# Selects between the early roots, an aggregate ahead of a scaling, and a first tap on GpSimd

## The reference

```python
x_sp = conv1d(x, conv_w, 3 taps, per channel, pad 1) + conv_b      # depthwise
x_mixed = x_sp^T @ lin_w^T + lin_b + emb.mean(0)                   # (16, 250, 128)
h = (x_mixed - mu) * rsqrt(var + 1e-5) * ln_g + ln_b

n1 = layernorm(h)
QK = (n1 @ Wq) @ (n1 @ Wk)^T
A = softmax(QK / 8); the row with the least sum of QK (of batch 0) is set to zero
h = h + A @ (n1 @ Wv)

n2 = layernorm(h)                                                  # over 128 features
h = h + tril(W2) @ gelu(tril(W1) @ n2 + b1) + b2
```

## Time and profile before

| | |
|---|---|
| median of 3 runs | 94.26 us (94.08 to 94.42) |
| profiled execution | 93.75 us |
| its span, first to last instruction | 92.0 us |
| TensorE busy | 85.0 us |
| VectorE busy | 73.6 us |
| ScalarE busy | 67.6 us |
| GpSimd busy | 54.9 us |
| granted TensorE clock | 1.000 |

### The profile page before, as it was taken

One profiled execution on the slowest core, in us unless ns is written; L12 is line 12 of the kernel. 1 busy time (PEld: TensorE's weight loads), 2 busy tenths in 40 slices (PEclk: granted clock), 3 DMA queues, 4 the chain that ended last, 5 costly groups with the idle time before them and its releaser, 6 DMA issues.

```text
span 92.0 us, 1984 instructions
## 1 busy us (share of the span) xinstructions
PE 85.0 (92%) x541; PEld 69.5 (76%) x541; DVE 73.6 (80%) x283; ACT 67.6 (73%) x241; POOL 54.9 (60%) x89
## 2 busy tenths in 40 slices
PE   5979987699999999999999999999999999999940
PEld 2446565379799989999899899989887988687730
DVE  2259999998999998999998899869769395862560
ACT  1688999999999769969787988666796735555400
POOL 5508768898856793999982079972708437460000
PEclk9999999999999999999999999999999999999999
DMA  1986000000000000000000000000000003425364
GB/s 23 218 289 200 0 0 4 4 0 0 11 0 0 0 0 0 0 7 4 4 0 0 0 0 7 0 0 0 0 0 0 0 7 111 115 69 154 108 188 150
DMA packets 3828, 3.84 MB, mean 42 GB/s; under 512 B 413, under 2 KB 3690, under 8 KB 3818
## 3 DMA queue, kind: packets, MB, share of 16 engines
q1 hardware_dynamic: 3466, 3.35, 13.1%
q10 hardware_dynamic: 352, 0.38, 1.4%
HBM read 1.68 MB, written 2.05 MB: 40 GB/s over the span
## 4 chain that ended last, share of the span: by engine, by line
PE 72%; DVE 8%; POOL 8%; DMA 3%; issue 3%; ACT 1%; POOLq 0%; DVEq 0%
PE bank_m L400 14%; PE bank_s L373 12%; PE bank_o L411 8%; PE bank_s L431 7%; PE bank_at L391 7%; PE bank_np L364 6%; PE bank_np L444 4%; PE bank_x L422 4%; POOL rstd L207 4%; DMA tok_w<-tok_dram 3%; PE bank_np L356 3%; PE bank_at L444 3%; POOL rstd_x L198 2%; DVE hb_all L774 2%; DVE bn L688 1%
## 5 line engine op out<-in xcount | busy, mean ns | idle before, releaser
L373 PE MATMUL bank_s<-n1t,pt 128*125 128x250 f32 x64 | 16.0, 375 | 0.5 <-ACT pt L565 0.5
L400 PE MATMUL bank_m<-at,n 125*128 125x250 f32 x64 | 16.2, 374 | 0.0
L570 ACT ACTIVATE a<-bank_s,neg_max 125x250 f32<-125x250 f32 x32 | 15.1, 479 | 0.7 <-DVE neg_max L711 0.7
L222 POOL TENSOR_TENSOR hb_all<-h_all,rows_sb 125x512 f32<-125x512 f32 x8 | 10.2, 1272 | 4.0 <-DVE h_all L747 4.0
L711 DVE TENSOR_REDUCE neg_max<-bank_s 125x2 f32<-125x500 f32 x16 | 10.7, 670 | 2.1 <-PE bank_s L373 2.1
L373 PEld LDWEIGHTS bank_s<-n1t,pt 128*125 128x125 f32 x64 | 11.0, 187 | 1.6 <-issue 0.6
L400 PEld LDWEIGHTS bank_m<-at,n 125*128 125x128 f32 x64 | 11.2, 190 | 0.9
L577 ACT ACTIVATE at<-bank_at 125x500 f32<-125x500 f32 x16 | 9.6, 597 | 1.9 <-PE bank_at L391 1.9
L207 POOL TENSOR_TENSOR rstd<-var_eps,neg_half 125x4 f32<-125x4 f32 (+2 forms) x11 | 9.5, 863 | 1.9 <-DVE var_eps L700 0.6
L364 PE MATMUL bank_np<-n1t,qk_w 128*128 128x250 f32 x32 | 9.6, 381 | 0.6 <-ACT n1t L559 0.6
L747 DVE SCALAR_TENSOR_TENSOR h_all<-bank_o,rinv_keep,h_all 125x128 f32<-125x128 f32 x32 | 9.6, 343 | 0.2
(11 more groups left out here) (121 smaller groups left out, 193.4 us busy)
## 6 DMA issues: line engine op xcount, KB each, us to landing
out_dram<-hb_all SPq DMA_DIRECT2D x7, 224.0 KB
x_all<-x_dram SPq DMA_DIRECT2D x8, 125.0 KB, 4.9
w_sb<-weights_dram SPq DMA_DIRECT2D x1, 320.5 KB, 5.7
out_dram<-hb_all SPq DMA_DIRECT2D x2, 112.0 KB
rows_sb<-rows_dram ACTq DMA_DIRECT2D x1, 187.5 KB
out_dram<-hb_all SPq DMA_DIRECT2D x6, 26.0 KB
tok_w<-tok_dram ACTq DMA_DIRECT2D x1, 130.0 KB, 3.1
out_dram<-hb_all ACTq DMA_DIRECT2D x2, 26.0 KB
```

Of the source, the lines that this page charges most:

```text
L222: pool.tensor_tensor(hb_all[:, j, :, :], h_tiles[:, j, :, :], b2_4, ALU.add).then_inc(hb_ready, 1)
L373: last = nc.tensor.matmul(s_ps[b % 2][:, a, :], pt[b % DEEP][:, a * H:(a + 1) * H], n1t[b % DEEP][:, :], start=True, stop=True)
L400: last = nc.tensor.matmul(mix_ps, n1[b // 2 % (HELD // 2)][:, 2 * (b % 2) + c, :], at_sb[b % DEEP][:, c, :], start=(c == 0), stop=(c == 1))
L570: ins = nc.scalar.activation(a_sb[b % DEEP][:, a, :], s_ps[b % 2][:, a, :], ACT.Exp, bias=neg_max[b % 2][:, a:a + 1], accum_out=exp_sum[:, ...
```

## The change

Three edits, all in the engines' lists of the head:

1. The first tap of pair 1 leaves ScalarE's list and becomes a `tensor_scalar` on GpSimd, at the front of its roots, with a semaphore of its own (`tap0_1_ready`). VectorE's `second_tap(1)` waits for that; the counts for later pairs go down by one.
2. On GpSimd `keep_triangles()` moves from behind `root_1(0, 1, 1)` to behind `root_x(0, 1, 1)`, ahead of `root_x(0, 2, 2)`.
3. On VectorE `aggregate_1(0, 2, 2)` (batch 1) moves ahead of `scale_x(1, 0, 2)` (pair 1, batch 2).

```diff
+            def first_tap_1():
+                pool.wait_ge(pads_zeroed, 2)
+                pool.wait_ge(landed_tok, 16)
+                pool.wait_ge(landed_x[1], 16)
+                pool.tensor_scalar(tap0[1][:, :], x_all[:, 1, 0:T], tok_w[:, D:D + 1], conv_b,
+                                   ALU.mult, ALU.add).then_inc(tap0_1_ready, 1)
...
-            root_x(0, 0, 1); root_x(0, 1, 1); root_x(0, 2, 2); root_1(0, 0, 1); root_1(0, 1, 1)
-            keep_triangles(); root_x(1, 0, 2); root_x(1, 2, 2); root_1(0, 2, 2); root_1(1, 0, 2)
+            first_tap_1(); root_x(0, 0, 1); root_x(0, 1, 1); keep_triangles(); root_x(0, 2, 2); root_1(0, 0, 1)
+            root_1(0, 1, 1); root_x(1, 0, 2); root_x(1, 2, 2); root_1(0, 2, 2); root_1(1, 0, 2)
...
             def first_tap(k):
-                if k == 1:
-                    act.wait_ge(pads_zeroed, 2)
                 act.wait_ge(landed_x[k], 16)
...
-            centre_lin(); centre_bias(); bias_hi(); first_tap(1); bias_mid(); square(0, 0); square(0, 1)
+            centre_lin(); centre_bias(); bias_hi(); bias_mid(); square(0, 0); square(0, 1)
...
                 if k == 0:
                     dve.wait_ge(tap0_0_ready, 1)
-                else:
-                    dve.wait_ge(tap0_ready, k)
+                elif k == 1:
+                    dve.wait_ge(tap0_1_ready, 1)
+                else:
+                    dve.wait_ge(tap0_ready, k - 1)
...
-            stats_1(0, 2, 2); scale_x(1, 0, 2); aggregate_1(0, 2, 2); head_h(1, 0, 2); stats_1(1, 0, 2)
+            stats_1(0, 2, 2); aggregate_1(0, 2, 2); scale_x(1, 0, 2); head_h(1, 0, 2); stats_1(1, 0, 2)
```

## The result

The changed kernel takes 94.88 us (94.50 to 96.28, 10 runs) against 94.27 (94.04 to 95.95, 10 runs): a ratio of 1.0063 with an interval of 1.0040 to 1.0085. It is slower, by 0.61 us, and lies 0.03 us above my range of 94.05 to 94.85.

What follows compares the result with a forecast made beforehand. TensorE was taken to bound the kernel from 24.92 us, so only its arrival there counted: 0 (ScalarE) + 0 (tap on POOL) + 0 (triangles) + 0.22 (DVE's order) = +0.22 us, giving 94.48 us, range 94.05 to 94.85.

Steps and rivals of the forecast that it cites:

- ScalarE's tap: Removing the 0.59 us tap from ScalarE only lengthens its 0.32 us wait before square(1, 0); gain 0.
- The tap on POOL: Tap at the front of GpSimd's roots: starts near 6.2, takes 0.4 us (0.37 to 0.71), cost 0.
- my worst case of 6.97: Latest start expected for VectorE's second_tap(1), 0.25 us late, if GpSimd's tap took its upper bound.
- Cost at the value taken: 0: With a 0.4 us tap on GpSimd, second_tap(1) begins at 6.65 instead of 6.72, delaying nothing; cost 0.
- Rival (a): Late GpSimd tap delays project_1 and what follows: 0.13 us on top of 0.22, 94.61 us, slower; chance 0.31.
- The selects: GpSimd's triangle selects, 0.77 us, moved ahead delay roots of pair 0 that have slack; cost and gain 0.
- The DVE's order: Moving VectorE's aggregate of batch 1 makes neighbours dependent, losing overlap twice: 0.22 us later from head_h on.
- GpSimd's cold start: GpSimd's add before root_1(1, 0, 2) takes 0.28 after waiting instead of 0.19; the 0.09 us was not charged.
- the gap ahead of root_1(1, 0, 2): GpSimd was expected to idle some 0.5 us or more before this root, whose add comes at 15.2.
- No later stretch gives it back: TensorE has no idle time behind 24.92 us, so any delay there reaches the end in full.
- Rival (b): VectorE's new order costs nothing and GpSimd's root still starts at 14.99: 94.26 us, no change; chance 0.22.
- Rival (c): An earlier project_1 or first_tap(3) in the head makes it faster, 93.93 us; chance 0.15.

Runs made afterwards that it cites:

- lean_tap_tri: Kernel before with the tap on GpSimd, the selects moved, VectorE's order unchanged, and four constant memsets moved from GpSimd to VectorE: 94.29 us, ratio 1.0003.
- tap_only: Kernel before with only the first tap of pair 1 moved to GpSimd, with its semaphore: 94.65 us, ratio 1.0037.
- tap_tri: Kernel before with the tap on GpSimd and the selects moved, VectorE's order left as it was: 94.41 us, ratio 1.0019.
- pad_pool: Kernel before, tap kept on ScalarE, with an unread one-column memset behind the tap's three waits at the tap's place on GpSimd: 94.63 us, ratio 1.0039.
- lean_full: The whole change plus four constant memsets moved from GpSimd's list to VectorE's, against the kernel before: 94.41 us, ratio 1.0010.
- order_only: Kernel before with only the aggregate of batch 1 moved ahead of scale_x(1, 0, 2) on VectorE: 94.46 us, ratio 1.0011.
- full_again: The whole change measured and profiled once more against the kernel before: 94.79 us, ratio 1.0065.

## Why the prediction was wrong

The forecast was +0.22 us, the measured +0.61. The sum that the runs bear out is 0.27 (the DVE's order) + 0.34 (a pause of GpSimd) = 0.61. The measured loss itself is known only to 0.38 to 0.80 us, so that the two agree to 0.01 is partly luck.

*ScalarE's tap: right.* Its wait of 0.32 us ahead of square(1, 0) wasn't even longer, because the freed time went into earlier waits (0.49 us for the DVE's cb_rest, ahead of bias_mid): nothing reached the end. The roots of pair 0, which I let start up to 0.3 us earlier, began at 7.30 as before.

*The tap on POOL: here is the step that failed.* The tap took 0.56 us, within my bounds of 0.37 to 0.71 though not near the low one. It began at 6.44, on a later landing of x, so second_tap(1) came at 7.03, past my worst case of 6.97. Even so the way that I had costed cost nothing: third_tap(1) ended at 8.16, project_1 stood behind qk_product until 8.56, and third_tap(1) releases project_1 in no chain that I read. The step that failed is "Cost at the value taken: 0". The edit costs 0.34 us through something that the sum had no term for: what stands behind it in GpSimd's list. No row of the kernel before showed it. Rival (a) had the sign and the edit, with 0.13 us by another mechanism; its mechanism didn't occur.

*The selects: right.* 12.39 and 0.9998.

*The DVE's order: mechanism right, size low by 0.05.* I took 0.03 us between a dependent scale and head_h, from a pair of stats and aggregate; it was 0.10. GpSimd's cold start, which I left out with a reason, was absent anyway: its add after waiting 0.80 us took 0.20. root_1(0, 2, 2) earlier brought nothing, and the gap ahead of root_1(1, 0, 2) was there (0.80, forecast 0.5 or more).

*No later stretch gives it back: right.* Both TensorE pieces moved by 1.40.

Rival (b) is excluded by the measured 0.27. Rival (c) needed an earlier head; in the changed kernel ScalarE still releases second_tap(3), behind the same wait for project_1, and lean_tap_tri, which has tap and selects without the two costs, is at 1.0003.

How much of the 0.61 is shown? The cost of the pause by three kernels besides the change that bring it (tap_only, tap_tri, pad_pool), and by lean_tap_tri and lean_full, in which it goes while the tap stays. The DVE's part is shown in the traces (0.27 in order_only and again in full_again) and is too small for the times alone. What GpSimd does in the pause stays open. A natural guess is a boundary between two parts of the list. The Trainium skill (Runtime: NRT & Kernel Launch, Instruction fetch mechanics) says that a list is fetched in blocks while the one before runs, and that crossing a boundary is mostly hidden. The ten profiles without a visible pause agree with "mostly hidden", the six with 0.33 to 0.36 us on the path don't. The transfers speak for a boundary. In the changed kernel's trace (the last column is GB/s):

```profile
22.00:22.50 0.50, 0.50 (x14) 0.50 (x11) 0.10 (x1) 0.50 (x3) 0.50 (x2) 1.00 0.13 33
24.00:24.50 0.50, 0.50 (x4) 0.46 (x5) 0.41 (x2) 0.50 (x6) 0.03 (x1) 1.00 0.00 0
25.00:25.50 0.50, 0.50 (x4) 0.38 (x2) 0.16 (x1) 0.50 (x3) 0.50 (x1) 1.00 0.06 16
```

The 33 GB/s behind 22 us are a transfer of 16,384 bytes in another queue, and nothing moves while the pause (24.08 to 24.52) lasts. But what moves at 25.15 is a transfer of instructions, 8,192 bytes. Every one of the sixteen traces has this transfer, 1.00 to 1.11 us behind the start of GpSimd's 68th entry (where that is the add behind a power, behind the start of the power), and in the six with the pause 0.62 to 0.66 us behind its end. It keeps to that entry whatever the kernel, so a boundary of the list lies there. The transfer begins only after the pause and can't be what GpSimd waits for. What it does wait for isn't known, and that the pause belongs to the boundary is an inference from their common place. Why the power of root_1(1, 0, 2) is held a second time in two of 16 profiles is open, too.

## What to carry to other kernels

An instruction added to an engine's list is paid not only where it runs: it shifts all that follows, and a pause that was hidden under a long operation can come to lie between two short dependent ones on the path. So test a move with a filling of the same length and no work (pad_pool) before believing a story about the work. Count the list's entries in the trace and not the lines of the source: one memset more or three waits more cost nothing here. And where GpSimd is critical, take constants out of its list when you put something in. On an engine without gaps, keep dependent neighbours apart: putting two dependent pairs together cost 0.27 us here, for a result that nobody was waiting for.

## What the runs showed of the hardware

- GpSimd has a pause of 0.33 to 0.36 us at one place of its list, behind the 68th recorded entry: between add and power (0.67 to 0.70 instead of 0.34, in five profiles of four kernels), or ahead of the add (0.46 instead of 0.14 to 0.15, in one). It can't be seen in the ten profiles in which GpSimd passes that place during a power of 1.0 us or more.
- Instructions are moved in transfers of 8,192 bytes in one queue and 16,384 in another; one of the first kind begins 1.00 to 1.11 us behind the start of that entry, or of the power in front of it, in all sixteen traces.
- A GpSimd instruction that reads SBUF is held while a DVE instruction with two SBUF inputs reads: the same power took 0.94 us beside one and 0.69 without. The Trainium skill (SBUF — State Buffer, Who interferes with whom) says so, and the traces agree; the DVE's instructions showed no lengthening. The power ended 0.55 us behind the end of the DVE instruction that held it.
- A tensor_scalar on GpSimd with two column operands took 0.56 us for 128x250, on the DVE 0.41 us.
- When the weights land varies from one execution to the next, in kernels with the same transfers: at 8 us TensorE waited 0.2 to 0.9 us for them in six profiles, and in ten no wait is shown. One profile of each kernel isn't a comparison; a distance between two events behind the landings is: it repeated within 0.03 us over the eight kernels without one of the two costs (12.39 to 12.42).
